# A four-layer graph network on one core: a scatter without a bound on its indices, and a block of zero rows written at a later place

## The reference, cut to what matters

```python
edge_index = jnp.stack([src, dst])          # 100000 edges, sorted by dst, 3125 nodes of 128 values
h = jnp.maximum(_layernorm(x), 0.0)
# layer 0: sums of edge_weight * (h @ W)[dst] over the edges of each SRC node, then batch norm
x = x + _L0_gnn_ref(h, W, bias, gamma, beta, edge_weight, src, dst)
#         msgs = edge_weight[:, None] * (feature @ weight)[edge_col]      edge_col = dst
#         agg  = segment_sum(msgs, edge_row, num_segments=N)              edge_row = src
# layer 1: sums of (h @ weight[rel])[src] over the edges of each dst node
# layer 2: graph attention over the edges of each dst node (softmax by dst)
# layer 3: transformer attention over the edges of each dst node, with edge features
```

## Time and profile before

| what | us |
|---|---|
| median of 3 runs | 4916.95 (4915.68 to 4922.77) |
| the profiled execution: its own time | 4933.33 |
| the profiled execution: span of the instructions | 4931.6 |
| mean granted TensorE clock | 0.709 |

### The profile page before, as it was taken

How to read it: one execution, slowest core, us unless ns; L and a number is a source line. 1 busy time by engine, 2 the same in 40 slices (tenths; PEclk the granted TensorE clock), 3 DMA queues, 4 the chain that set the end, 5 groups by cost and what they waited for, 6 DMA issues and landing times.

```text
span 4931.6 us, 58738 instructions
## 1 busy us (share of the span) xinstructions
PE 3108.3 (63%) x17717; PEld 2647.6 (54%) x17717; DVE 2379.7 (48%) x5597; ACT 924.0 (19%) x2143; POOL 3239.5 (66%) x3283
## 2 busy tenths in 40 slices
PE   6765444554496444344445888887885777777776
PEld 5654333444493333333334777776773565666664
DVE  9742222222374000100003666666665888888886
ACT  3211111110002443333331111111111111111111
POOL 2267777777400777777774777777772777777773
PEclk7565777655698555555555777778777899899998
DMA  3511111111482111111111222222221333333332
GB/s 100 174 43 52 52 51 51 50 50 50 157 298 115 53 53 52 50 53 53 53 53 48 55 55 54 55 55 55 55 54 50 102 99 100 100 100 100 100 101 61
DMA packets 162124, 377.42 MB, mean 77 GB/s; under 512 B 59963, under 2 KB 72132, under 8 KB 160892
## 3 DMA queue, kind: packets, MB, share of 16 engines
q0 software_dynamic: 118656, 276.72, 19.4%
q1 hardware_dynamic: 38706, 94.06, 5.4%
q10 hardware_dynamic: 4474, 2.92, 0.2%
HBM read 292.49 MB, written 83.61 MB: 76 GB/s over the span
## 4 chain that ended last, share of the span: by engine, by line
POOL 57%; issue 19%; PE 13%; DVE 7%; DMA 3%; DVEq 1%; POOLq 0%; ACT 0%; ACTq 0%; SPq 0%
POOL work L625 26%; POOL work L609 16%; POOL msgs L594 15%; PE banks L1011 4%; PE banks L844 2%; PE banks L808 1%; PE banks L827 1%; PE banks L919 1%; PE banks L834 1%; DMA work<-kv_table,idx_a 1%; PE banks L909 1%; DVE scores L1279 1%; DVE acc L1188 1%; DVE acc L1281 1%; DMA work<-gat_table,idx_a 1%
## 5 line engine op out<-in xcount | busy, mean ns | idle before, releaser
L609 POOL DMA_INDIRECT work<-rel_table,idx_b x808 | 770.8, 954 | 543.4 <-DMA rel_table<-work 297.4
L625 POOL DMA_INDIRECT work<-kv_table,idx_a x808 | 820.7, 1016 | 296.2 <-issue 241.2
L625 POOL DMA_INDIRECT work<-gat_table,idx_a x808 | 800.4, 991 | 291.1 <-issue 242.0
L594 POOL DMA_INDIRECT msgs<-work,idx_a x808 | 786.2, 973 | 291.2 <-issue 244.6
L1059 PE MATMUL banks<-work,arena 128*128 128x128 f32 x1616 | 414.8, 438 | 591.7 <-DMA work<-rel_table,idx_b 583.4
L1059 PEld LDWEIGHTS banks<-work,arena 128*128 128x128 f32 x1616 | 356.6, 325 | 656.0 <-issue 656.0
L1000 PE MATMUL banks<-nodes,work 128*128 x1616 | 355.4, 389 | 458.7 <-DVE work L1502 458.7
L844 PE MATMUL banks<-work,arena 128*128 128x136 f32 x3232 | 564.3, 328 | 58.7 <-DVE work L1210 56.5
L1000 PEld LDWEIGHTS banks<-nodes,work 128*128 128x128 f32 x1616 | 305.5, 283 | 525.6 <-issue 525.6
L844 PEld LDWEIGHTS banks<-work,arena 128*128 128x128 f32 x3232 | 506.7, 231 | 124.3 <-issue 113.9
L682 ACT ACTIVATE attr<-banks 128x512 f32<-128x512 f32 x404 | 241.2, 597 | 1450.3 <-PE banks L819 1450.3
(11 more groups left out here) (300 smaller groups left out, 4618.7 us busy)
## 6 DMA issues: line engine op xcount, KB each, us to landing
work<-msgs SPq DMA_DIRECT2D x101, 516.0 KB, 4.6
msgs<-work,idx_a POOLq DMA_INDIRECT x808, 2.3
work<-rel_table,idx_b POOLq DMA_INDIRECT x808, 2.5
work<-gat_table,idx_a POOLq DMA_INDIRECT x808, 2.5
work<-kv_table,idx_a POOLq DMA_INDIRECT x808, 2.7
rel_table<-work SPq DMA_DIRECT2D x25, 512.0 KB, 2.6
attr<-in_edge_attr SPq DMA_DIRECT2D x50, 250.0 KB
rec<-work SPq DMA_DIRECT2D x1, 6400.0 KB, 18.4
```

Source lines behind the costliest of these rows:

```text
L594: nc.gpsimd.indirect_dma_start(msgs, bass.IndirectOffsetOnAxis(ap=idx_a[:, t:t + 1], axis=0), msg_ring[:, t % SPAN, :], None, bounds_check ...
L609: nc.gpsimd.indirect_dma_start(row_ring[:, t % SPAN, :], None, rel_table, bass.IndirectOffsetOnAxis(ap=idx_b[:, t:t + 1], axis=0)).then_in ...
L625: nc.gpsimd.indirect_dma_start(ring[:, t % SPAN, :], None, table, bass.IndirectOffsetOnAxis(ap=idx_a[:, t:t + 1], axis=0)).then_inc(quad_i ...
```

## The change

The scatter of line 594 loses its bound, and `msgs` grows to twice its rows. The empty place of partition p in tile t now gets the index PLACES + p x T + t, a row in the second half of the array that belongs to it alone and that nothing reads; it is therefore written. For this, DVE adds p x T + PLACES to the tile numbers `tile_no` once, and takes that array in place of the constant PLACES in the last steps of the index computation. The gap scatters of line 551 keep their bound. The wait for `gap_out` and the tail DMA are moved on POOL from ahead of the group gathers to behind them.

```diff
-        msgs = dram("msgs", [PLACES, MSG])
+        msgs_all = dram("msgs", [2 * PLACES, MSG])
+        msgs = msgs_all[0:PLACES, :]
...
-            pool.wait_ge(gap_out, 16 * NB)
-            pool.dma_start(msgs.rearrange("(p t) w -> p t w", t=T)[:, MG_T:T, :],
-                           rep(bn[:, :, :].rearrange("p a f -> p (a f)")[:, 0:MSG], T - MG_T)).then_inc(tail_out, 16)
             pool.wait_ge(flag_set, 1)
...
                     bass.IndirectOffsetOnAxis(ap=group_i[0:k, c:c + 1], axis=0),
                     bounds_check=GROUPS - 1, oob_is_err=False).then_inc(group_in[c], 16)
 
+            pool.wait_ge(gap_out, 16 * NB)
+            pool.dma_start(msgs.rearrange("(p t) w -> p t w", t=T)[:, MG_T:T, :],
+                           rep(bn[:, :, :].rearrange("p a f -> p (a f)")[:, 0:MSG], T - MG_T)).then_inc(tail_out, 16)
             pool.wait_ge(tail_out, 16)
             for q in range(NQ_FULL):
                 pool.wait_ge(quad_rdy, q + 1)
                 for t in range(QUAD * q, QUAD * (q + 1)):
                     nc.gpsimd.indirect_dma_start(
-                        msgs, bass.IndirectOffsetOnAxis(ap=idx_a[:, t:t + 1], axis=0),
-                        msg_ring[:, t % SPAN, :], None, bounds_check=PLACES - 1, oob_is_err=False)\
-                        .then_inc(quad_out[q % QUADS], 16)
+                        msgs_all, bass.IndirectOffsetOnAxis(ap=idx_a[:, t:t + 1], axis=0),
+                        msg_ring[:, t % SPAN, :], None).then_inc(quad_out[q % QUADS], 16)
...
+            V.tensor_scalar(vio[:, 1:2], node_no[:], float(T), float(PLACES), ALU.mult, ALU.add)
+            drain()
+            V.tensor_scalar(tile_no, tile_no, vio[:, 1:2], None, ALU.add)
             for i in range(0, 4 * TC, 2):
                 field_out(V.tensor_copy, dve, i)
...
-            V.scalar_tensor_tensor(fields[:, 0, :], fields[:, 0, :], -float(PLACES), map_tmp, ALU.add, ALU.mult)
-            drain()
-            V.tensor_scalar(idx_a[:, 0:T], fields[:, 0, :], float(PLACES), None, ALU.add).then_inc(tiles_set, 1)
+            V.tensor_tensor(fields[:, 0, :], fields[:, 0, :], tile_no, ALU.subtract)
+            drain()
+            V.tensor_tensor(fields[:, 0, :], fields[:, 0, :], map_tmp, ALU.mult)
+            drain()
+            V.tensor_tensor(idx_a[:, 0:T], fields[:, 0, :], tile_no, ALU.add).then_inc(tiles_set, 1)
```

## The result

Over 20 runs each, the changed kernel has a median of 4914.70 us (4907.10 to 4922.28), the kernel before 4928.46 us (4915.68 to 4939.37). The ratio of the two is 0.9975 with a 95% interval of 0.9967 to 0.9983, so 12.3 us faster (8.4 to 16.3 us: the bounds times 4928.46); the medians alone differ by 13.8 us. The forecast was 27.6 us, and the median lies above the range given, whose upper end was 4912. The direction was right, the size forecast was more than twice the measured one. The profiled execution has a span of 4909.7 us; 4931.6 of before less that is 21.9 us.

The account below looks back on a forecast made before the run. The prediction took POOL's 808 scatters at a 1.278 us cadence to bound the scatter stage, with the preparation second. Its terms, -7.1 + 0 + 1.5 - 22 = -27.6 us, took the median of 4916.95 to 4889.3 us; range 4875 to 4912.

Parts of the forecast that it names:

- Part 1: Preparation: without the tail DMA beside the feature loads, DVE's copy of line 1375 starts 7.1 us earlier.
- Part 2: Preparation's end: the tail behind the group gathers is covered before the first scatter; cost 0, bounds 0 to 2 us.
- Rival D: Preparation: the moved tail is not covered or disturbs the gathers, taking back 2 to 7 us; chance 0.10.
- Part 3: Index computation on DVE before the first scatter: longer last steps cost 1.5 us, the two new instructions are hidden.
- Part 4: Scatter stage: dropping the bound saves 28 ns on each of 808 scatters, taken as 22 us.
- rival A: Scatter stage: the bound is free, only the preparation gains 5.6 us, giving 4911.3 us; chance 0.13.
- Rival C: Scatter stage: unbounded scatters lose their even beat to DVE, mean 1016 ns, giving 4946 us; chance 0.04.

Follow-up runs that it names:

- f1: The kernel before with only the tail DMA and its wait moved behind the group gathers: 4922.45 us, ratio 0.9976.
- f3: The changed kernel with a bound that no index exceeds put back on the scatter, empty places still written: 4931.11 us, ratio 0.9994.
- e6: The changed kernel with message rows of 128 values (512 bytes) in place of 129, right sums left out: 5524.83 us.
- f2: The changed kernel with the tail DMA and its wait put back at their old place: 4928.67 us, ratio 0.9986.
- e4: The changed kernel with a bound that no index exceeds on the 808 gathers of line 609: 5525.45 us.
- f5: The changed kernel with the first one-hots computed ahead of the index computation: 4917.57 us, ratio 0.9970.
- e7: The kernel before with the tail DMA issued twice at its old place, on other, slower chips: 5568.10 us beside 5552.48.
- e0: The changed kernel without an edit, on other chips where the kernel before is slower: 5523.74 us, ratio 0.9945.
- e1: The kernel before with only the tail DMA and its wait moved behind the group gathers, on other, slower chips: 5541.93 us, ratio 0.9980.
- e3: The changed kernel with a scatter bound that no index exceeds, on other, slower chips: 5544.48 us beside 5552.48.

## Why the prediction was wrong

*Part 1, the old place of the tail: right.* The forecast was 7.1 us, 5.9 to 7.15, and f1 moves the first scatter by 6.9 us. The order of limits held too: PE's waits go, and then the end of the ranks on DVE sets the time.

*Part 2, the new place: right, 0.* Rival D falls. The gathers land about as before and the tail behind them; it took 30.1 us, not 23.4, and it started while the gathers filled the engines (1.02 at 215 to 219 us). By the Trainium skill ("DMA: Bandwidth & Descriptors", "Two DMAs through the same engine are not ordered"), descriptors within one queue of one DMA engine start in order. The trace agrees: the tail, issued at 215.8 us behind the gathers, made PE wait no longer for them.

*Part 3, the index: right.* 1.5 us were forecast, 3.09 - 1.58 = 1.51 measured, and the two new instructions are hidden in DVE's gap.

*Part 4, the bound: the step that failed.* The prediction took the whole 28 ns between the bounded scatter and the unbounded gather as the bound's and made 22 us of it. The bound is 14 of them (972 to 958; f3 puts them back), the other 14 remain on a scatter without a bound, at 512 bytes too (e6). In these two executions the stage gained less again, 11 ns per scatter, since more scatters were long: 13 above 1.05 us for 3 before, worth 2.8 against 0.7 us, that is 2.7 ns per scatter (counted in the timelines of both). This count is partly chance: with a bound it is 3 (before), 7 (f1) and 11 (f3), without one 13 and 16 (f2). So the term is 8.6 us (1031.0 - 1022.4; 8.5 from f3 and f2), and the sum becomes -7.1 + 1.5 - 8.6 = -14.2 us, inside the measured 8.4 to 16.3. The prediction had asked the right question, bound or direction, but answered it with line 585, which is a gather. By e4 this row was near the truth for gathers (48 ns by the row, 53 measured) and told nothing of scatters. The two causes of the 28 ns were treated as either-or, with 22 us for the one and 0 (rival A) for the other; the truth was half of each. On the median of 4916.95 that gives 4903 (4916.95 - 14.2 = 4902.75), a time that no case of the list stood at. The upper end of the range was rival A's time on the three runs' median of 4916.95; over 20 runs the median of before is 11.5 us higher. With it the forecast sum gives 4900.9 and the corrected one 4914.3. So that the time fell outside the range is partly this; that the gain was half the forecast is not.

*Rival C: its mechanism is there, its size not.* Three places in the changed kernel, the scatters between DVE's instructions:

```profile
699.52 0.69 DVE L1505 TENSOR_TENSOR work<-banks,arena 128x512 f32<-128x512 f32 x1 [3.69 <-DMA msgs<-work,idx_a]
699.67 0.95 POOL L595 DMA_INDIRECT msgs<-work,idx_a  x1 [0.31 <-issue]
700.19 0.69 DVE L1494 TENSOR_TENSOR work<-iota,dst_local 128x512 f32<-128x512 f32 x1
700.93 0.96 POOL L595 DMA_INDIRECT msgs<-work,idx_a  x1 [0.30 <-issue]
...
918.44 0.69 DVE L1494 TENSOR_TENSOR work<-iota,dst_local 128x512 f32<-128x512 f32 x1
918.50 1.46 POOL L595 DMA_INDIRECT msgs<-work,idx_a  x1 [0.30 <-issue]
...
1095.95 0.69 DVE L1494 TENSOR_TENSOR work<-iota,dst_local 128x512 f32<-128x512 f32 x1
1096.12 1.35 POOL L595 DMA_INDIRECT msgs<-work,idx_a  x1 [0.31 <-issue]
```

At 700 the one-hot (line 1494) starts inside one scatter and ends 0.05 us before the next: nobody is longer. At 918.50 and 1096.12 the scatter starts while the one-hot runs, and is longer by 0.50 and 0.39 us, nearly what is left of it (0.63 and 0.52). These are no chosen cases. In six traces together (before, the changed kernel, f1, f2, f3, f5), each of the 66 scatters that start with at least 0.25 us of a one-hot left takes what is left plus 0.82 to 0.85 us. Of the 1001 that start with as much left of DVE's multiplication (line 1500 or 1505, one input in SBUF and one in `banks`, the other on-chip memory, as at 699.52) none but the first of a kernel takes over 1.00 us. The Trainium skill's rule ("SBUF — State Buffer", "Who interferes with whom"), that a VectorE instruction with two SBUF inputs contends with a GpSimd instruction that reads SBUF, fits these rows. The prediction dismissed it on the mean of the earlier trace rows, in which the 3 long ones of that execution do not show. It costs as much as the phase between the two engines makes it cost: 2.8 us here, 5.9 in f5, where it took back most of what the earlier start gave.

## What to carry to other kernels

Where a stage is nothing but one engine's instructions in a row, price an edit on the same kind of instruction: a gather's row says little of a scatter. Where two rows differ in two things, their difference is a bound for each and not a price, and the likeliest case may be that each has a share. This bulk DMA on one queue held up the loads of another: look for what waits beside such a DMA, and put it where nobody waits. Earlier or faster starts in a stage like this shift the phase of two engines that get in each other's way, so read the number of long instructions, not only the median.

## What the runs showed of the hardware that was not expected

A bound costs a scatter of 128 rows 14 ns (972 against 958) and a gather of 128 rows 53 ns (1000 against 947). A bounded scatter also has one register instruction of 29 ns on POOL's queue, 808 in all, that an unbounded one has not; the time ahead of the scatters is the same with it and without (244.6 and 244.8 us over 803 of them).

One DMA of 2257.5 KB in rows of 516 bytes took 23.4 us beside the feature loads. One 250 KB load of the other queue stood 18.99 us beside it, and two such DMAs held PE up for 22.8 us (e7).

A scatter that starts with at least 0.25 us of a one-hot of DVE left takes what is left plus 0.82 to 0.85 us; a one-hot that starts inside a scatter lengthens neither (rows at 700 us above).

On the chips of the first series PE often stood idle without a wait that the profile shows. The waits of the scatter stage in e0, beside those of the changed kernel on the first chip:

```profile
PE banks L1000 <- issue: 454.0, 372, 3.8
...
POOL msgs L595 <- DVE work L1507: 140.4, 34, 6.2
```
```profile
PE banks L1000 <- DVE work L1507: 432.4, 183, 3.8
...
POOL msgs L595 <- DVE work L1507: 45.3, 3, 44.7
```

On the first chip PE waits for DVE, that is for the ring, and POOL waits for DVE only at the start. In e0 PE stands 372 times with no releaser but issue, and POOL waits 34 times for DVE. There the stage took 1183.5 us with the bound (e1), 1184.2 with the wide bound (e3) and 1164.6 without (e0), 19 us less. The scatters' own durations do not explain it: their median is 9 ns lower without the bound (962 against 971), but their mean is 3 ns higher (977 in e0, 974 in e1). What shrank is POOL's waiting for DVE, from 200.2 us in e1 to 182.6 in e0, the wait ahead of the first scatter included. That the 808 register instructions fewer let the others come sooner there would fit; no run takes it apart, and it stays open.
